# The end of the attention phase in another order: last inverses, row sums, weighing, exponentials and the turned logits

## The reference

```
x = x + attention(layernorm(x), ctx)      # x: 32 x 256 x 256, ctx: 32 x 120 x 256, 16 heads of 16
xn = rmsnorm(layernorm(x))                # 8192 tokens x 256
logits = (xn * norm_weight) @ router.T + bias         # 16 experts
idx = the 512 tokens with the largest logit, for each expert
y[e] = gelu(xn[idx[e]] @ fc1[e].T + b1[e]) @ fc2[e].T + b2[e]
x = x + (sum of y, weighed with the softmax of the logits and divided by the sum of the weights)
```

## Time and profile before

| | us |
|---|---|
| median of 3 runs | 975.06 (974.56 to 977.03) |
| the profiled execution | 970.46 |
| its span, first to last instruction | 968.7 |
| TensorE busy in the span | 848.8 (88%) |
| VectorE busy | 742.9 (77%) |
| GpSimd busy | 594.6 (61%) |
| ScalarE busy | 510.7 (53%) |
| attention phase ends, first instruction of the search | 483.76 |

### The profile page before, as it was taken

One profiled execution on the slowest core, in us unless ns is written; L12 is line 12 of the kernel. 1 busy time (PEld: TensorE's weight loads), 2 busy tenths in 40 slices (PEclk: granted clock), 3 DMA queues, 4 the chain that ended last, 5 costly groups with the idle time before them and its releaser, 6 DMA issues. The chain is left out here.

```text
span 968.7 us, 20968 instructions
## 1 busy us (share of the span) xinstructions
PE 848.8 (88%) x6115; PEld 727.1 (75%) x6115; DVE 742.9 (77%) x1659; ACT 510.7 (53%) x929; POOL 594.6 (61%) x562
## 2 busy tenths in 40 slices
PE   8799999999999999998611149999999999999995
PEld 6578888878888888886501137989999999999985
DVE  5588888888888888876598856988777777777642
ACT  4555565556655665565165107465555555555531
POOL 4266666677666766666342255588887776775345
PEclk9999999999999999999755559999999999999998
DMA  5466566566665665554141033466666556665333
GB/s 173 162 226 213 195 213 221 201 199 213 226 204 195 211 225 201 195 189 143 65 145 44 8 104 118 136 198 171 165 168 162 157 159 162 159 174 149 97 72 43
DMA packets 129508, 156.49 MB, mean 162 GB/s; under 512 B 22448, under 2 KB 104624, under 8 KB 129344
## 3 DMA queue, kind: packets, MB, share of 16 engines
q1 hardware_dynamic: 104064, 113.05, 35.9%
q0 software_dynamic: 15616, 25.70, 12.3%
q10 hardware_dynamic: 9792, 17.31, 4.9%
HBM read 74.93 MB, written 26.28 MB: 104 GB/s over the span
## 5 line engine op out<-in xcount | busy, mean ns | idle before, releaser
L583 DVE TENSOR_REDUCE NM<-bank 128x4 f32<-128x480 f32 x256 | 155.4, 649 | 60.6 <-PE bank L741 60.5
L414 ACT ACTIVATE PT<-bank 120x512 f32<-120x512 f32 x256 | 142.8, 603 | 36.6 <-PE bank L766 35.4
L342 POOL TENSOR_SCALAR XN<-X,mv,rstd 128x256 f32<-128x256 f32 x124 | 150.9, 1226 | 14.2 <-POOL rstd L337 13.3
L1656 PE MATMUL bank<-W2H,HH 128*128 128x256 f32 x512 | 144.8, 283 | 2.0 <-issue 2.0
L1658 PE MATMUL bank<-W2H,HL 128*128 128x256 f32 x512 | 143.6, 280 | 0.0
L1657 PE MATMUL bank<-W2L,HH 128*128 128x256 f32 x512 | 143.5, 280 | 0.0
L1117 POOL DMA_INDIRECT out_dram<-C,IO x60 | 111.3, 1855 | 50.7 <-issue 31.0
L1385 DVE TENSOR_TENSOR HL<-hf,HH 128x512 fp32r<-128x512 f32 x128 | 87.3, 690 | 49.8 <-ACT HH L1540 49.1
L766 PE MATMUL bank<-QX,KX 128*120 128x256 f32 x512 | 110.0, 307 | 9.4 <-DMA QX<-NMT 5.7
L541 DVE RECIPROCAL RR<-RC 128x256 f32<-128x256 f32 x64 | 111.5, 1743 | 6.3 <-DMA RC<-PVS 6.3
L1535 ACT ACTIVATE hf<-bank,B 128x512 f32<-128x512 f32 x128 | 87.9, 687 | 40.6 <-PE bank L1658 34.9
(11 more groups left out here) (192 smaller groups left out, 1888.4 us busy)
## 6 DMA issues: line engine op xcount, KB each, us to landing
QX<-QH ACTq DMA_DIRECT2D x64, 256.0 KB
W<-w1T_dram SPq DMA_DIRECT2D x16, 1024.0 KB, 5.5
W<-w2T_dram SPq DMA_DIRECT2D x16, 1024.0 KB, 5.8
X<-x_dram SPq DMA_DIRECT2D x32, 256.0 KB, 3.2
QX<-QL SPq DMA_DIRECT2D x32, 256.0 KB
XB<-x_dram SPq DMA_DIRECT2D x32, 256.0 KB, 2.8
RC<-PVS SPq DMA_DIRECT2D x64, 128.0 KB, 2.1
OC<-PVS SPq DMA_DIRECT2D x64, 128.0 KB, 2.3
```

The lines of the kernel that those rows point to most:

```text
L342: ins = pool.tensor_scalar(dst[:, t, :], src[:, t, :], mv[:, t, 0:1], rstd[:, t:t + 1], ALU.subtract, ALU.mult)
L414: act.activation(PT[u][0:M, HE * k:HE * (k + 1), :], score_bank(b, k // 2)[k % 2][0:M, :], ACT.Exp, scale=SCALE) \
L583: dve.tensor_reduce(NM[u][:, t, :].rearrange("p (f n e) -> p n e f", n=HN, e=HE)[:, n, :, :], smax_bank[q % 2][:, 0:4 * M].rearrange("p (e ...
L1656: pe.matmul(o, wh, xh, start=first, stop=False)
```

## The change

Seven edits, all in the last steps of the attention phase:

- ScalarE: XN2T of batch 28 is copied in step 32, behind PVS, and no longer in step 31 between the exponentials.
- SP: the store of XN2(29) moves from step 31 to step 32, behind the row sums of batch 31.
- VectorE: in step 32 the two inverses of batch 31 stand next to each other, in front of batch 30's residual.
- GpSimd: in steps 31 and 32 the bias and the weighing stand in front of the variances and the normalising.
- TensorE: 28 matmuls of `keep_clock` and not 16.
- The logits are turned in groups 0 to 3, 4 and 5, 6 and 7 (steps 33, 34, 35), and not in groups 0 to 5 and 6 and 7 (steps 34, 35). `row_maxima` follows: three pieces and not two.
- `odd_logits` moves from step 35 to step 34.

```diff
--- before.py
+++ after.py
@@ -40,7 +40,7 @@
 NCONST = 6
 GMAX = float(CAP) - 0.5
 ROUNDS = 8
-CLOCK = 16
+CLOCK = 28
 ALONE = 2
 HT = CT // 2
 SMAX = GMAX - NC * HT / 2
@@ -108,7 +108,7 @@
 
     LT, LPF, odd, _, (not_sign, even) = search_views(search_tiles)
     LP, mx = LPF.rearrange("p (j q) -> p j q", j=TC), search_tiles[3]
-    EARLY = TC - TB
+    EARLY, LATE = TC - 2 * TB, TC - TB
 
     smax_bank = bank[0:2]
     logits_t = bank[0:2]
@@ -287,20 +287,24 @@
                     sp.dma_start(out[bass.ds(b, 1), :, :].rearrange("o (t p) d -> p (o t) d", p=P),
                                  X1[u][:, :, :]).then_inc(x1_stored[u], 16)
 
-            def store_xn2():
-                b, u, j, live = batch(i, c, 2)
+            def store_xn2(off):
+                b, u, j, live = batch(i, c, off)
                 if live:
                     hold(xn2_ready, b + 1)
                     sp.dma_start(xn_table.rearrange("(p t) d -> p t d", t=NT)[:, bass.ds(TB * b, TB), :],
                                  XN2[u][:, :, :]).then_inc(xn2_stored[u], 16)
 
+            last = 2 * i + c - (B - 1) if known(i) else -B
             low_queries()
             attended()
+            if last == 1:
+                store_xn2(3)
             store_x1()
             residual()
             rows()
             context()
-            store_xn2()
+            if last != 0:
+                store_xn2(2)
             clear_maxima()
             keys(2, KL, kl_ready)
             row_sums(0)
@@ -382,10 +386,14 @@
             last = 2 * i + c - (B - 1) if known(i) else -B
             deviations(-2, mv1, ve1, rstd1, 1.0, EPS, stats1_ready, ve1_ready, rstd1_ready)
             rows1()
+            if last in (0, 1):
+                residual()
+                attended()
             deviations2(2)
             rows2()
-            attended()
-            residual()
+            if last not in (0, 1):
+                attended()
+                residual()
             if last == -1:
                 search_constants(pool, search_const, *search_consts)
 
@@ -474,8 +482,8 @@
                     wait(act, kx_moved[u], 16 * 6 * j)
                     act.activation(KH[u][:, :, :], key_bank[:, 0:HE * M], ACT.Copy).then_inc(kh_ready, 1)
 
-            def rows2():
-                b, u, j, live = batch(i, c, 3)
+            def rows2(off):
+                b, u, j, live = batch(i, c, off)
                 if live:
                     act.wait_ge(xn2T_done, b + 1)
                     wait(act, logit_done, b - 1)
@@ -485,7 +493,10 @@
                         ins = act.activation(XN2T[u][:, k, :], xn2_bank[:, k * S:(k + 1) * S], ACT.Copy, scale=nw_sb[:, k:k + 1])
                     ins.then_inc(xn2T_ready, 1)
 
+            last = 2 * i + c - (B - 1) if known(i) else -B
             keep_pv(1, pvs1_ready)
+            if last == 1:
+                rows2(4)
             maxima()
             move_high(-1, 0)
             keys()
@@ -496,15 +507,18 @@
             exp(3)
             exp(4)
             exp(5)
-            rows2()
+            if last != 0:
+                rows2(3)
             rows()
             exp(6)
             exp(7)
             keep_pv(0, pvs0_ready)
-            if known(i) and 2 * i + c == B + 2:
+            if last == 2:
                 act.wait_ge(lt_done, 1)
-                act.activation(LT[:, 0:P * 4], logits_t[0][:, :], ACT.Copy).then_inc(lt_ready, 1)
-                act.activation(LT[:, P * 4:P * EARLY], logits_t[1][:, 0:P * (EARLY - 4)], ACT.Copy).then_inc(lt_ready, 1)
+                act.activation(LT[:, 0:P * EARLY], logits_t[0][:, :], ACT.Copy).then_inc(lt_ready, 1)
+            if last == 3:
+                act.wait_ge(lt_done, 2)
+                act.activation(LT[:, P * EARLY:P * LATE], logits_t[1][:, 0:P * (LATE - EARLY)], ACT.Copy).then_inc(lt_ready, 1)
             queries()
             move_high(-2, 2)
 
@@ -625,21 +639,25 @@
 
             last = 2 * i + c - (B - 1) if known(i) else -B
             row_sums(0)
+            if last == 1:
+                row_sums(1)
             residual()
-            if last == 4:
-                odd_logits()
             keep_logits()
             if last == 2:
+                turn_logits(B - 2, 0, EARLY)
                 last_rows()
+                row_maxima(0, TB * (B - 2))
             if last == 3:
-                turn_logits(B - 1, 0, EARLY)
-                row_maxima(0, TB * (B - 1))
+                turn_logits(B - 1, EARLY, LATE)
+                odd_logits()
+                row_maxima(TB * (B - 2), TB * (B - 1))
             if last == 4:
-                turn_logits(B, EARLY, TC)
+                turn_logits(B, LATE, TC)
                 row_maxima(TB * (B - 1), TB * B)
-                dve.wait_ge(lt_done, 2)
-                dve.tensor_copy(LT[:, P * EARLY:CT], logits_t[1][:, P * (EARLY - 4):P * 4]).then_inc(lt_ready, 1)
-            row_sums(1)
+                dve.wait_ge(lt_done, 3)
+                dve.tensor_copy(LT[:, P * LATE:CT], logits_t[1][:, P * (LATE - 4):P * 4]).then_inc(lt_ready, 1)
+            if last != 1:
+                row_sums(1)
             low_keys()
             for q in range(4):
                 row_max(q)
@@ -860,8 +878,10 @@
             rows2()
             scores(5)
             rows()
+            if last == 2:
+                turn_logits(1, 0, EARLY)
             if last == 3:
-                turn_logits(1, 0, EARLY)
+                turn_logits(2, EARLY, LATE)
             max_scores(2)
             scores(6)
             max_scores(3)
@@ -882,9 +902,9 @@
             weigh(3)
 
         run(pe, step, -2, 4)
-        pe.wait_ge(lp_ready, 2)
+        pe.wait_ge(lp_ready, 3)
         pe.wait_ge(lt_ready, 2)
-        for j in range(EARLY, TC):
+        for j in range(LATE, TC):
             ins = pe.transpose(logits_t[j // 4][:, P * (j % 4):P * (j % 4 + 1)], LP[:, j, :], ident[:, :])
         ins.then_inc(lt_done, 1)
```

## The result

The changed kernel takes 968.79 us, the median of 6 runs (966.46 to 970.99), against 975.04 of 6 runs of the kernel before (972.02 to 977.74): ratio 0.9935, 95% interval 0.9911 to 0.9958, or 6.25 us less. The forecast was 970.4, with 967.0 to 973.0 as its range and 0.81 on faster. Timed again, beside 11 runs of the kernel before, it took 967.46 (ratio 0.9926, 0.9909 to 0.9943).

What follows compares the result with a forecast made beforehand. The prediction took the serial chain of batch 31 at attention's end, before the search, as the bound. Search moves from 483.76 to 479.14, 4.6 us less, subtracted from the 975.06 median: 970.4 us, range 967.0 to 973.0.

Steps and rivals of the forecast that it cites:

- The chain: End of attention: batch 31's row sums, inverses, weighing, projection, residual, statistics, XN2(31), transposes, router, search; search 4.6 us earlier.
- The side branch: GpSimd step 31: XN2(29) normalised after weighing 30, ending at 460.8 instead of 458.44, covered by TensorE's queue.
- The exponentials' 0.71: ScalarE step 31: moving the XN2T(28) copies makes exponentials 6 and 7 and both PVS copies 0.71 us earlier.
- the weighing's place: GpSimd step 32: weighing 31 before batch 30's variances and normalising, starting at 463.77 instead of 468.50, 4.7 us earlier.
- the store's move: SP's queue: XN2(29)'s store leaves the place before RC, which goes at 457.95, not 458.91; needed since XN2(29) comes later.
- the tail from XN2(30) on: TensorE's last transposes and routers, all priced at 1.2 GHz: XN2(30) at 469.24, last router ending at 477.01.
- rival A: TensorE's clock stays at 2.4 GHz through the tail; search about 476.7, gain 7.0 us, 968.0 us; chance 0.17.
- B, late inverses: Inverses of 31 come late, GpSimd and VectorE wait; gain only 2 to 2.6 us, about 972.7; chance 0.14.
- C, projection at 1.2 GHz: TensorE's projection of 31 takes 3.45 us instead of 1.99; gain 3.8 us, 971.3 us; chance 0.05.
- D, slower through the experts: Shifted work meets a lower TensorE clock at the experts' start; over 978 us, needing 7.5 us lost; chance 0.04.
- Costs taken as nothing: Extra logit copy and maxima hidden on VectorE (up to 1.2 us uncovered); 28 matmuls free, at worst a few tenths.
- The shared ports: VectorE's first logit copy and GpSimd's work for 31 may block each other: XN2(31) up to 0.4 us later, sum unchanged.

Runs made afterwards that it cites:

- u_act: Changed kernel with XN2T of batch 28 copied between the exponentials again; second inverse of batch 30 to search 25.24 us (changed kernel 23.81).
- u_pool: Changed kernel with GpSimd's old order (variances and normalising before weighing and bias); second inverse of batch 30 to search 30.90 us (changed 23.81).
- u_sp: Changed kernel with the store of XN2(29) ahead of batch 31's row sums on SP again; second inverse of batch 30 to search 29.03 us (changed 23.81).
- b_weigh: Kernel before with only GpSimd's new order and batch 31's inverses together; second inverse of batch 30 to search 28.88 us (before 30.15).
- n_both: Changed kernel with VectorE normalising batch 30 and 8 plus 3 unread matmuls; stretch to search 23.19 us, time 966.04 us, ratio 0.9901 to the kernel before.
- n_dve30: Changed kernel with VectorE normalising batch 30 as well as 31; second inverse of batch 30 to search 23.84 us (changed 23.81).
- a_again: Changed kernel profiled again, no edit; second inverse of batch 30 to search 24.27 us (first profile 23.81).
- u_clock: Changed kernel with 16 matmuls of keep_clock, not 28; second inverse of batch 30 to search 23.77 us (changed 23.81).
- u_groups: Changed kernel with logits turned in two groups, odd_logits and maxima at their old places; second inverse of batch 30 to search 24.79 us (changed 23.81).
- n_clock: Changed kernel with 12, 3 and 3 unread matmuls in three TensorE pauses; second inverse of batch 30 to search 23.43 us (changed 23.81).
- u_dve: Changed kernel with batch 30's residual between the two inverses of batch 31 again; second inverse of batch 30 to search 23.90 us (changed 23.81).
- b_again: Kernel before profiled again, unchanged; second inverse of batch 30 to search 30.10 us (first profile 30.15).

## Why the prediction was right, and which term was off

All in microseconds behind the anchor; forecast times less 453.61, measured ones less 457.09.

| step | forecast | measured |
|---|---|---|
| PVS half 0 copied | 4.30 | 4.29 |
| RC issued | 4.34 | 4.31 |
| first inverse of 31 | 6.54 | 6.46 |
| weighing of 31 | 10.16 | 9.91 |
| projection of 31, start and duration | 11.47, 1.99 | 11.35, 1.89 |
| residual of 31 | 13.50 | 13.28 |
| XN2(30) ends | 15.63 | 15.48 |
| XN2(31) ends | 17.4 | 17.37 |
| router of 30 ends | 19.62 | 18.18 |
| router of 31 ends | 23.40 | 21.68 |
| search | 25.53 | 23.81 |

**The chain was right link by link down to XN2(31)**, within 0.25 us. The side branch was later than forecast: XN2(29) ended 7.67 us behind the anchor and not 7.19, because GpSimd came free later. The exponentials' 0.71 is shown by u_act, the weighing's place by u_pool, and the statement that the store's move is needed because XN2(29) comes later is shown by u_sp and b_weigh. The order of the last links was right too: XN2(30) and its router are in front of XN2(31) on TensorE; with XN2(30) early in n_both the transposes of 31 came 0.5 us earlier.

**The mis-sized term is the tail from XN2(30) on, above all its clock.** I had priced everything there at 1.2 GHz: 7.77 us from XN2(30) to the end of the last router, measured 6.20. Of the 1.57, 1.29 lie up to the end of batch 30's router and 0.28 behind it. By rows, transposes and router of batch 30 ran at 2.4 GHz and give 0.46 (0.66 for 1.12) and 0.69 (1.06 for 1.75). The transposes of batch 31, half at 2.4 GHz, give 0.29 (0.83 for 1.12), and the last router takes back 0.14 (1.89 for 1.75).

The remaining 0.28 is no clock but a row misread: I took 1.07 us from the end of the transposes to the router as ScalarE's copies and the weight load, twice. It is 0.93 both times here, at either clock. The kernel before had it too, at batch 30, where the router waits 0.93 us after transposes that end at 474.55; its 1.07 at batch 31 had six transposes queued in front of the router:

```profile
475.48 1.25 PE L838 MATMUL bank<-rw_sb,XN2T 128*128 128x16 f32 x8 [0.93 <-ACT XN2T L485]
478.11 1.49 PE L819 MATMUL bank<-ident,hf 128*128 128x128 f32 x6
```

Together with 0.15 from the links before, this is the 1.7 by which 4.6 became 6.3. The truth lies between the forecast and rival A, which had the whole tail at 2.4 GHz and 7.0, so that the range held owes something to A's having been counted in. The argument "from 476.2 on TensorE worked almost without a break, yet the router took 1.75" came from one execution of another kernel, in which the clock had been down during the projection as well; it could not place the fall after the change. Over the runs whose projection of 31 ran at 2.4 GHz the clock fell in the router of batch 30 (u_act, n_dve30), at or in the transposes of batch 31 (changed, a_again, u_clock), right in front of the six transposes of the logits behind them (u_groups), in the last router (n_both), behind it (n_clock), or not before the last transposes were done (u_dve). Why it falls in one place and not in another is open; the fillings of n_clock and n_both went with late falls, but so did u_dve, which has none of them.

**Rivals.** B, late inverses: RC landed as before, 2.15 us from issue to the inverse's start (2.20 before), and nothing was lost. Its mechanism is real, though: u_sp makes RC 3.6 us late, and both chains move with it. C, projection at 1.2 GHz: not in the changed kernel, but in u_sp, u_pool and b_weigh (3.56, 3.63, 3.68), where TensorE paused 3.6 to 4.5 us; after pauses of 1.19 (u_clock) and 1.75 us (u_dve) it ran at 2.4 GHz (1.99, 2.00). D, slower through the experts: from the search to the end the changed kernel took 483.8 us and the kernel before 484.9 and 483.9, so no loss. The clock at the start of the experts that D went by, 0.80 over the earlier trace rows, is 0.90 at the same distance from the search in the changed kernel, and in b_again too: it differs between executions of the kernel before. The last section has the spread of the whole stretch.

**Costs taken as nothing.** The three groups and `odd_logits` were not only free; undoing them costs 1.0 us. I had counted only the 0.5 of `odd_logits`; the four transposes that leave the place in front of the last router are the other half. The 28 matmuls cost next to nothing in the first profile (they end at 468.60, OT(31) at 468.29, and the projection starts at 468.44), but 0.95 us at the projection in a_again and 0.76 in n_clock, more than the few tenths allowed for. They stand behind the transposes of batch 29, so they end late when XN2(29) comes late: I had it 0.5 us too early, and it differs between executions. No run shows a gain from the 12 added ones.

XN2(31) had 0.66 us to spare in front of TensorE and not 2, since batch 30's transposes and router were shorter, and in a_again nothing: there the transposes of 31 start 0.06 us after XN2(31) ends.

**The shared ports.** GpSimd's variances of batch 31 met the first logit copy in several runs. In a_again, VectorE and GpSimd:

```profile
473.04 0.43 DVE L626 COPY hf<-L 128x512 f32<-128x512 f32 x1
```

```profile
473.12 0.39 POOL L339 TENSOR_SCALAR ve<-mv 128x2 f32<-128x2 f32 x1 [0.67 <-DVE mv L545]
```

The variances take 0.39 and not 0.19, and end 0.04 after the copy does. u_sp, u_dve and n_clock repeat it with 0.39, u_pool, n_both and n_dve30 with 0.38; in the changed kernel's first profile they start later in the copy and take 0.24, and in u_groups, with no copy there, 0.19. By the Trainium skill (SBUF — State Buffer, "SBUF: two separate sides") GpSimd is blocked until the copy ends. The trace agrees, in that the variances never end before the copy. At most 0.20 us is lost, half of the 0.4 allowed for; the sum for the first profile did not change, as XN2(31) had time to spare there.

## What to carry to other kernels

In a drain the last item should pass every in-order queue first, ahead of the work of the item before it; but edits like these stand in series on different engines, and each is worth little until the others are made: GpSimd's and VectorE's orders alone gave 1.27 us, all together 6.34, and undoing GpSimd's alone lost 7.09. When one engine's order makes a tile later, look for the queue in which something urgent stands behind that tile's store. And measure such a change from an instruction that both traces share, not from the start of the span, and judge it with several profiles where the clock of TensorE can fall in the stretch.

## What the runs showed of the hardware

Two executions of the same program differ by more than the change's smaller parts. The anchor stood between 453.6 and 457.9 us, and the two low values had a mean clock near 1.00 from 20 to 30 us (1.00 at 453.61, 0.96 at 454.03), the others 0.76 to 0.83 but for u_pool, which had 0.96 and still 456.30, so this is not the whole of it.

From the search to the end the runs took 483.6 to 484.9 us, 485.0 to 485.3, or 486.7 to 487.2. All five of the last group (u_act, u_dve, n_both, n_dve30, b_weigh) had a mean clock of 0.92 between 108 and 130 us behind the search, where those under 485 had 1.00. The middle group doesn't line up: u_sp 1.00, u_clock and n_clock 0.94, and u_pool 0.92 with 485.3, so this window is at most a part of it. These windows of n_both and of a_again:

```profile
588.13:610.13 22.00, 21.96 (x127) 19.52 (x128) 13.32 (x27) 11.56 (x18) 14.12 (x13) 0.92 0.34 108
```

```profile
589.21:611.21 22.00, 22.00 (x142) 20.10 (x143) 15.01 (x37) 11.57 (x18) 13.79 (x14) 1.00 0.40 135
```

TensorE is busy throughout in both and completes 127 matmuls in one and 142 in the other. What lets the clock fall there in some executions was not tried. The spread behind the search, 3.6 us, is larger than what any single edit here is worth except GpSimd's and SP's.
